# A four-layer conditioned feed-forward kernel: the first step of the third layer's rounding on ScalarE for four of eight tiles

## The reference, cut to what matters

```python
def activation_quant(x, num_bits=8):
    s = qp / jnp.clip(jnp.max(jnp.abs(xf), axis=-1, keepdims=True), EPS, None)
    return (jnp.clip(jnp.round(xf * s), qn, qp) / s).astype(x.dtype)
...
h = jax.nn.silu(bit_linear(x, w_gate)) * bit_linear(x, w_up)
h = rms_norm(h, ln_weight)
return bit_linear(h, w_down)
```

## Time and profile before

| | |
|---|---|
| runs, us | 900.35, 897.52, 899.87 (median 899.87) |
| profiled execution, its own time | 899.28 us |
| its span, first to last instruction | 897.6 us |
| mean granted TensorE clock | 0.931 |
| busy share | PE 85%, PEld 64%, DVE 64%, ACT 49%, POOL 27% |
| third layer's rounding, by the start and end of the groups of line 1551 | 318.8 to about 348.5 us of the span |
| instructions | 11277 |

### The profile page before, as it was taken

The page is one execution under the profiler, slowest core; times in us unless marked ns, Lnnn a source line. Parts: engine busy times, 40 slices in busy tenths (PEclk is TensorE's granted clock), DMA queues, the critical chain, the costliest instruction groups (busy, mean ns, idle before and its releaser), DMA issues.

```text
span 897.6 us, 11277 instructions
## 1 busy us (share of the span) xinstructions
PE 759.3 (85%) x3633; PEld 576.1 (64%) x3633; DVE 577.1 (64%) x1285; ACT 437.8 (49%) x878; POOL 240.5 (27%) x245
## 2 busy tenths in 40 slices
PE   1886785978785555799999999999969999999997
PEld 0433453634453134688888988888857888888885
DVE  5998889879988896556566566755664233232233
ACT  5895452235414646456455555654654334334342
POOL 5310112320140623011021021201111455555553
PEclk9999897789896878899999999999997999999998
DMA  4000003923222000210110101101010632323421
GB/s 149 2 1 1 0 0 111 381 66 106 82 71 70 1 0 1 94 48 1 48 39 11 47 1 48 37 1 37 1 38 11 154 95 59 95 46 73 93 55 47
DMA packets 37422, 49.84 MB, mean 56 GB/s; under 512 B 18574, under 2 KB 29942, under 8 KB 35702
## 3 DMA queue, kind: packets, MB, share of 16 engines
q1 hardware_dynamic: 36310, 46.90, 17.1%
q0 software_dynamic: 768, 2.10, 0.7%
q10 hardware_dynamic: 288, 0.14, 0.1%
HBM read 42.99 MB, written 6.13 MB: 55 GB/s over the span
## 4 chain that ended last, share of the span: by engine, by line
PE 59%; DVE 7%; ACT 2%; issue 1%; POOL 1%; DVEq 0%; ACTq 0%
PE bank L2000 15%; PE bank L2566 10%; PE bank L2016 8%; PE bank L2580 5%; PE bank L2561 5%; PE bank L2655 3%; PE bank L2638 3%; PE bank L2645 2%; PE bank L2656 2%; PE bank L2637 1%; PE bank L1614 1%; PE bank L1717 1%; DVE H L1551 1%; DVE XC L324 1%; DVE H L1530 1%
## 5 line engine op out<-in xcount | busy, mean ns | idle before, releaser
L2044 DVE TENSOR_TENSOR B_l<-bank,TW_l 128x512 f32<-128x512 f32 (+1 forms) x50 | 34.5, 691 | 134.3 <-PE bank L2000 131.3
L2211 POOL TENSOR_TENSOR WL<-RAW,WH 128x512 fp32r<-128x512 f32 x32 | 41.8, 1312 | 232.4 <-ACT WH L2244 232.4
L2069 POOL TENSOR_TENSOR HL_l<-H_l,HH_l 128x512 fp32r<-128x512 f32 (+1 forms) x50 | 64.9, 1298 | 121.9 <-ACT HH_l L2061 121.9
L2302 ACT ACTIVATE EX<-EX,nm 128x128 f32<-128x128 f32 (+1 forms) x128 | 57.0, 446 | 72.6 <-DVE nm L2453 72.6
L2053 ACT ACTIVATE S_l<-bank 128x512 f32<-128x512 f32 (+1 forms) x50 | 29.9, 599 | 86.1 <-PE bank L2000 85.9
L159 POOL TENSOR_TENSOR WV<-EUK,V 128x512 f32<-128x512 f32 x16 | 23.8, 1495 | 152.6 <-DVE GAIN L274 89.9
L2467 DVE TENSOR_TENSOR AL<-bank,AH 128x256 fp32r<-128x256 f32 x64 | 27.2, 424 | 56.6 <-ACT AH L2316 56.6
L2566 PE MATMUL bank<-XH,WH 128*128 128x512 f32 x128 | 60.3, 471 | 3.7 <-DVE XL L1766 2.8
L2000 PE MATMUL bank<-XH,WH 128*128 128x512 f32 (+1 forms) x136 | 55.0, 405 | 0.0
L2000 PE MATMUL bank<-XL,WH 128*128 128x512 f32 (+1 forms) x136 | 54.5, 401 | 0.0
L2000 PE MATMUL bank<-XH,WL 128*128 128x512 f32 (+1 forms) x136 | 54.5, 401 | 0.0
(11 more groups left out here) (319 smaller groups left out, 2198.5 us busy)
## 6 DMA issues: line engine op xcount, KB each, us to landing
RAW<-l_attn SPq DMA_DIRECT2D x8, 1024.0 KB, 4.8
WE<-l_experts SPq DMA_DIRECT2D x1, 6144.0 KB, 22.8
TW_l<-routed SPq DMA_DIRECT2D x14, 256.0 KB, 4.2
RAW<-l_w SPq DMA_DIRECT2D x3, 1024.0 KB
RAW<-l_experts SPq DMA_DIRECT2D x6, 512.0 KB, 3.9
TW_l<-routed SPq DMA_DIRECT2D x14, 192.0 KB, 3.3
sorted_x<-ZERO SPq DMA_DIRECT2D x1, 1920.0 KB, 8.0
XIN<-sorted_x SPq DMA_DIRECT2D x15, 128.0 KB, 2.2
```

The lines of the kernel that those rows point to most:

```text
L2069: pool.tensor_tensor(self.HL[0:rows, q % 4], self.H[0:rows, q % 2], self.HH[0:rows, q % 4].bitcast(F32), ALU.subtract).then_inc(self.h_low, 1)
L2211: pool.tensor_tensor(WL[g % 2][:, c], RAW[g % 2][:, c], WH[g % 2][:, c].bitcast(F32), ALU.subtract).then_inc(w_low, 1)
L2302: act.activation(EX[:, s, a:b], EX[:, s, a:b], ACT.Exp, bias=nm[:, s, i:i + 1], scale=scale, accum_out=rs[:, s, i:i + 1]).then_inc(expd, 1)
```

## The change

A second column beside the epsilon constant holds ROUND, filled by a second memset on POOL, and `roots` waits for both. For tiles 0 to 3 the step of line 1551 leaves DVE; a new function `scaled(u)` does the same arithmetic in place on ACT, as an Identity activation with the factor s2 as its scale and the constant as its bias, both of them read from a column of 128 values. ACT's queue gets scaled(0) and scaled(1) behind gates(6), scaled(2) behind gates(7), and scaled(3) behind roots(1). DVE's queue keeps its order; its `rounds(u)` for these tiles is now a wait for `hr` and the instruction of line 1555. Tiles 4 to 7 stay as they are.

```diff
@@ -1360,7 +1360,8 @@
-        EPS = sb("EPS2", [P, 1], F32)
+        CONST = sb("EPS2", [P, 2], F32)
+        EPS, MAGIC = CONST[:, 0:1], CONST[:, 1:2]
@@ -1415,7 +1416,8 @@
         def gpsimd(pool):
-            pool.memset(EPS[:], 1e-6).then_inc(made, 1)
+            pool.memset(EPS, 1e-6).then_inc(made, 1)
+            pool.memset(MAGIC, ROUND).then_inc(made, 1)
@@ -1449,9 +1451,9 @@
             def roots(n):
 
-                act.wait_ge(made, 1)
+                act.wait_ge(made, 2)
                 act.wait_ge(sq, parts[n].stop)
-                act.activation(rt[:, parts[n]], ss[:, parts[n]], ACT.Sqrt, bias=EPS[:], scale=1.0 / FF2).then_inc(root, 1)
+                act.activation(rt[:, parts[n]], ss[:, parts[n]], ACT.Sqrt, bias=EPS, scale=1.0 / FF2).then_inc(root, 1)
@@ -1466,6 +1468,13 @@
+            def scaled(u):
+
+                act.wait_ge(post, 6)
+                act.wait_ge(lnd, u + 1)
+                act.wait_ge(hmx, u + 1)
+                act.activation(H[:, u], H[:, u], ACT.Identity, bias=MAGIC, scale=s2[:, u:u + 1]).then_inc(hr, 1)
@@ -1478,12 +1487,17 @@
             roots(0)
-            for u in range(LATE2):
-                t = EARLY2 + u
-                gates(t)
-                product_turned(u)
-                squares(t)
+            gates(EARLY2)
+            scaled(0)
+            scaled(1)
+            product_turned(0)
+            squares(EARLY2)
+            gates(EARLY2 + 1)
+            scaled(2)
+            product_turned(1)
+            squares(EARLY2 + 1)
             roots(1)
+            scaled(3)
             for u in (LATE2, LATE2 + 1):
                 product_turned(u)
                 out(u)
@@ -1548,7 +1562,9 @@
             def rounds(u):
-                v.tensor_scalar(H[:, u], H[:, u], s2[:, u:u + 1], ROUND, ALU.mult, ALU.add).then_inc(hr, 1)
+                if u >= 4:
+                    v.tensor_scalar(H[:, u], H[:, u], s2[:, u:u + 1], ROUND, ALU.mult, ALU.add).then_inc(
+                        hr, 1)
                 v.wait_ge(hr, u + 1)
                 if u >= 2:
                     v.wait_ge(turnh, u - 1)
```

## The result

The changed kernel takes 902.4 us (median of 10 runs, 901.74 to 903.21), the kernel before 899.64 us (median of 10, 897.52 to 901.69). The ratio is 1.0031, with a 95% interval of 1.0022 to 1.0041: 2.8 us slower. That is small, but the interval leaves out 1, so the slowdown is real. The forecast was 900.9 us, with a range of 898.7 to 902.8 us. The profiled execution took 902.88 us, with a span of 901.1 us, 3.5 us more than the span before.

A forecast was written before the change was run, and what follows sets the result against it. A passage between two layers, with DVE nearly full, was taken as the bound; moving work to ACT delays tile 3's clamp by 1.03 us, 0.47 of it at tile 0. Forecast 900.9 us beside the 899.87 median, range 898.7 to 902.8 us.

The forecast's parts named there:

- a clock that stays down: Rival: products of tiles 1 to 3 at PE's lower level lose one more product and a transpose, 902.2 us; chance 0.14.
- one meeting of 0.5 us: POOL's multiplication for tile 7 beside DVE's line 1551: counted as nothing, 0.5 us more as upper end.
- The price on ACT: An Identity of 128x1024 f32 with two columns on ACT: 1.23 us, 1.13 us from start to next start.
- First link: Tile 0: scaled(0) on ACT ends later than DVE's step did, so the clamp of tile 0 starts 0.47 us later.
- Second link: ACT's queue from tile 7's second Silu to scaled(3): the clamp of tile 3 starts 1.03 us later in all.
- "Both are shifted alike, so nothing is absorbed": Where DVE had waited 0.32 us for PE at 337.53: both sides move by 1.03 us, so no slack helps.
- the rival to which I had given 0.12: PE's clock stays up for tile 3's transposes and product(2): 1.25 us comes back, 899.7 us; chance 0.12.
- The sum: Profiled execution: 899.28 + 1.03 = 900.3 us; beside the median of 899.87, a forecast of 900.9 us.
- table load appeared ahead of an Identity: Rival on ACT: Identity needs its own table loads of 1.28 us, some 4.9 us on top, 905.8 us; chance 0.04.
- DVE's relief: Rival: ACT delivers each tile in time and line 1551's 3.6 us leaves the path, 896.5 us; chance 0.04.
- Nothing was absorbed: Rival: the shift is absorbed later in the passage or in the fourth layer, 899.9 us; chance 0.12.

The follow-up runs named there:

- with tile 3 on DVE: Changed kernel with tile 3 scaled on DVE again, tiles 0 to 2 staying on ACT: 901.78 us, ratio 1.0024.
- POOL's hold for the factors: Changed kernel with POOL's four weight remainders of the fourth layer held until DVE's second set of factors is through: 901.89 us, ratio 1.0014.
- the hold until all tiles are rounded: POOL's weight remainders held until all eight tiles are rounded: 897.47 us, ratio 0.9982, on the kernel before; 895.49 us, ratio 0.9978, on the changed one.
- The repeated maximum: Kernel before, with DVE taking the maximum of tile 6 a second time ahead of tile 7's, nothing moved to ACT: 903.07 us, ratio 1.0033.
- The two repeats at 900.6 us: The changed kernel itself, unaltered, profiled a second and a third time: 900.58 and 900.64 us, one run each.
- the four versions with that hold: POOL held until all tiles are rounded: kernel before 0.9982, changed 0.9978, ACT scaling tiles 2 to 5 instead 0.9975, changed with scaled(3) before the square root 0.9984.
- One kernel's runs: Changed kernel with POOL's weight remainders held until DVE's second factors are through, twelve runs: median 901.89 us, ratio 1.0014.

## Why the forecast held in its range and was short in its size

The measured median lies inside the range, 0.4 us below its upper end, and just past what I called telling from no change. That it fell inside is in part luck: the upper end was made for a clock that stays down and for one meeting of 0.5 us, and neither is what happened. Step by step:

- **The price on ACT** was right: 1.230 us measured against 1.23 us. Two of them back to back cover 2.37 us, so 1.14 us from start to start against 1.13.
- **First link**: the clamp of tile 0 moved from 7.50 to 8.05 on the ruler, 0.55 us; forecast 0.47.
- **Second link**: the clamp of tile 3 moved by 0.91 us; forecast 1.03. The order of the chain was the forecast's. DVE stood idle for 2.24 us there; the forecast had some 2.9 us. HT of tile 2 and POOL's multiplication for tile 7 stayed covered: the clamp took 0.69 us.
- **"Both are shifted alike, so nothing is absorbed"** is the step that failed. PE's side was not shifted: its transposes and product ran at the higher clock level, the rival to which I had given 0.12, in all three profiles of the changed kernel (0.62 and 1.04 us by the timeline; 1.03 and 1.91 us in both of the kernel before). What PE did ahead of that had moved too: product(1) waits for the later HT and ends 3.5 us ahead of the transposes in place of 3.8, as the rival had it. That this is why the clock stayed up isn't shown. On the ruler POOL's subtractions start at 25.16, 25.52 and 25.00 us in the changed kernel, at 25.49 and 25.39 before, so they did not move back with the clamp. I let that rival give its 1.25 us back to the sum, as if PE's side were the path. It wasn't; DVE's was, and what PE's being in time did was to keep ACT's conversions and POOL's subtractions from moving with DVE. Where PE ran at the lower level, with tile 3 on DVE, all of it did shift alike, and nothing was added.
- **The missing term** is what the late DVE meets there. I had read POOL's row beside line 1551 and priced one such meeting, at tile 7, at 0.5 us; the four subtractions at 337.53 were not asked after, though the residual at 337.53 and the stretched rounding step at 338.74 (1.84 us) stood right behind it in the same timeline. Cost: 0.98 us, less 0.32 us of slack. This is shown by taking it away: POOL's hold for the factors gives 1.03 us back on the ruler, and the hold until all tiles are rounded leaves 0.40 of the 1.60 us. The repeated maximum shows that the stretching needs nothing of the change. The Trainium skill (SBUF — State Buffer, SBUF: two separate sides) describes it: the port pair that DVE shares with GpSimd is an exclusive lock. GpSimd wants it, and so does a DVE instruction in a 2-port mode or, where the GpSimd instruction reads SBUF, one with two SBUF inputs; the side that comes second waits until the other's instruction is through. By that rule a 128x2 instruction that meets a subtraction of 1.26 to 1.33 us waits as long as a large one would, and one with a single input outside such a mode doesn't. The trace agrees in the times: 1.25, 1.20, 0.98 and 1.30 us for the four stretched ones, 0.17 us for the reciprocal among them. In which mode a DVE instruction ran no trace here shows.
- **The sum.** 0.91 + 0.98 - 0.32 = 1.57 us are shown, where the profile has 1.60 and the medians are 2.8 us apart. The rest of the profile's difference lies behind the conditioned tile, all of it in the first 57 us with the clock at 0.84 in place of 0.85; of three profiles two show it and one the opposite, at 0.89. Whether the changed kernel meets the low clock more often there, or these ten runs did so by chance, stays open. That the ten runs all fell in 901.74 to 903.21 us speaks for the former. The two repeats at 900.6 us speak for the latter only in part: one has the shorter rest, the other an earlier start of the passage.
- **The other rivals**: no table load appeared ahead of an Identity. DVE's relief counted for nothing (6.93 of 12.70 us busy, and waiting). Nothing was absorbed.

## What to carry to other kernels

When an engine comes later by some time, look at what runs there on the engine with which it shares a resource, and not only at what it delays: here 0.9 us of lateness cost 1.6. What counts is how many instructions meet it, not how large they are: each lost about 1 us, four small ones 4.02 us and three large ones 3.04 us. Before moving work to an engine with idle time, look for the idle stretch itself (ACT had 6.4 us before 321 us and 4.4 us before 334) and for what stands ahead in its queue: a table load and a square root that the receiver didn't need cost 1.9 us of the clamp's start here. And holding POOL's weight work back by one semaphore wait, an edit outside the change, gave a ratio of 0.9982 (0.9968 to 0.9995) in the kernel before, and 3.0 us on the ruler; the four versions with that hold lie at 0.9975 to 0.9984.

## What I had not expected of the hardware

- A DVE instruction on 128x2 numbers takes up to 1.30 us beside POOL's 128x512 subtractions, against 0.22 us alone, while a reciprocal of the same size among them takes 0.17 us.
- POOL pays less than DVE: its four subtractions cover 4.94 us with POOL held until the rounding is over, 4.93 us when they meet the small instructions, and 5.85 us with the large ones in the kernel before.
- What goes with the clock is larger than most edits: with the same DVE instructions behind it, the time from the conditioned tile to the end ranges over 8.7 us between profiles, and the granted clock of its first 57 us from 0.74 to 0.89. One kernel's runs fall into two heaps 3 us apart (898.1 to 898.8 and 901.7 to 902.9 us). The one profiled is of the lower heap and has the 0.94 from 318 us on, worth about 3 us; that the upper heap lacks it is likely but not shown. A difference of 1 us in this kernel is seen on a ruler inside the trace and not in a median of ten runs.
